# Expert tile lists with full tiles first, and list padding written from ScalarE's queue inside the tile loop, in a fused graph-attention and mixture-of-experts kernel

## The reference

```python
x = x + gnn(layernorm(x), adj, a0, a1, a2, a3)        # x is [128, 128, 128] f32
x = x + ffn(layernorm(x), gate_w, gate_b, w1, w2, w3)

# gnn: e_k = leaky_relu(einsum('bid,bjd->bij', h * a_k, h), 0.2); alpha takes e_k where adj == k + 1,
#      else -9e15; softmax over j; alpha @ h
# ffn: 16 experts, hidden 256
logits = einsum('bsd,de->bse', x, gate_w) + gate_b
probs = softmax(logits)
top_probs, top_idx = top_k(probs, 2)
top_probs = top_probs / sum(top_probs)
hidden = silu(x @ w1[e]) * (x @ w2[e])                # for each chosen expert e
out = sum over the two chosen e of top_prob_e * (hidden @ w3[e])
```

## Time and profile before

| | |
|---|---|
| median of 3 runs | 967.29 us (967.28 to 970.02) |
| the profiled execution | 967.5 us |
| its span in the trace | 965.7 us |
| busy, share of the span | PE 78%, POOL 54%, DVE 65%, ACT 45% |
| mean granted TensorE clock | 0.92 of full |
| bytes moved | 160.39 MB |

### The profile page before, as it was taken

The page is one execution under the profiler, slowest core; times in us unless marked ns, Lnnn a source line. Parts: engine busy times, 40 slices in busy tenths (PEclk is TensorE's granted clock), DMA queues, the critical chain, the costliest instruction groups (busy, mean ns, idle before and its releaser), DMA issues.

```text
span 965.7 us, 17975 instructions
## 1 busy us (share of the span) xinstructions
PE 748.7 (78%) x4233; PEld 594.5 (62%) x4233; DVE 624.6 (65%) x2534; ACT 438.3 (45%) x1090; POOL 521.3 (54%) x571
## 2 busy tenths in 40 slices
PE   2677677777777777420939999999959999999995
PEld 1344444444444444410729999888848999999995
DVE  2799999999999999740516666666533444444442
ACT  3687777777777777310303333333313333333331
POOL 2025555555555555550316666667654666766665
PEclk9899999999999999755869999999989999999998
DMA  3223333322222211113768878777728888888882
GB/s 104 72 82 100 99 100 100 100 83 70 68 67 68 67 56 35 33 46 91 250 240 269 281 272 271 250 264 259 245 84 272 271 265 273 275 267 269 270 268 86
DMA packets 134202, 160.39 MB, mean 166 GB/s; under 512 B 16985, under 2 KB 103263, under 8 KB 134144
## 3 DMA queue, kind: packets, MB, share of 16 engines
q1 hardware_dynamic: 117248, 125.37, 41.5%
q0 software_dynamic: 16896, 34.40, 10.5%
HBM read 55.53 MB, written 47.62 MB: 107 GB/s over the span
## 4 chain that ended last, share of the span: by engine, by line
SPq 38%; issue 13%; POOL 2%; DMA 2%; DVE 1%; PE 1%; ACT 0%; POOLq 0%; DVEq 0%
SPq L331 10%; SPq L328 9%; SPq L332 9%; SPq L329 7%; SPq L319 2%; SPq L320 2%; POOL second_list L425 1%; POOL out_dram L437 1%; POOL first_list L413 0%; DMA xin<-second_list 0%; PE bank L819 0%; DMA xin<-first_list 0%; DMA first_list<-padding 0%; SPq L326 0%; DMA first_list<-stage,slot 0%
## 5 line engine op out<-in xcount | busy, mean ns | idle before, releaser
L847 PE MATMUL psS<-xT,late 128*128 128x256 f32 x1280 | 308.4, 384 | 2.2 <-ACT xT L519 2.1
L847 PEld LDWEIGHTS psS<-xT,late 128*128 128x128 f32 x1280 | 234.0, 193 | 29.9 <-issue 2.0
L425 POOL DMA_INDIRECT second_list<-xin x160 | 156.9, 981 | 132.2 <-issue 66.3
L733 DVE TENSOR_TENSOR hid<-silu,psS 128x512 f32<-128x512 f32 x160 | 109.9, 687 | 161.5 <-PE psS L847 156.8
L437 POOL DMA_INDIRECT out_dram<-xin x160 | 156.5, 978 | 87.8 <-issue 66.5
L515 ACT ACTIVATE silu<-psS 128x512 f32<-128x512 f32 x160 | 95.5, 597 | 224.1 <-PE psS L847 224.1
L767 PE MATMUL psS<-late,hT 128*128 128x512 f32 x256 | 145.7, 721 | 44.5 <-ACT late L468 44.5
L868 PE MATMUL bank<-late,hid 128*128 128x128 f32 x1280 | 170.1, 276 | 0.1
L413 POOL DMA_INDIRECT first_list<-stage,slot x128 | 137.3, 1073 | 60.6 <-DVE stage L611 28.7
L868 PEld LDWEIGHTS bank<-late,hid 128*128 128x128 f32 x1280 | 156.5, 193 | 0.5 <-issue 0.4
L405 POOL TENSOR_TENSOR norm<-veps,minus_half 128x8 f32<-128x8 f32 (+1 forms) x36 | 55.5, 1541 | 154.9 <-DVE veps L584 154.9
(11 more groups left out here) (111 smaller groups left out, 820.3 us busy)
## 6 DMA issues: line engine op xcount, KB each, us to landing
late<-wts SPq DMA_DIRECT2D x160, 384.0 KB
xin<-second_list SPq DMA_DIRECT2D x80, 262.0 KB
xin<-first_list SPq DMA_DIRECT2D x80, 134.0 KB
X<-in_x_dram SPq DMA_DIRECT2D x32, 256.0 KB, 4.0
late<-in_adj_dram SPq DMA_DIRECT2D x32, 256.0 KB, 3.5
wts<-in_L_ffn_w_dram SPq DMA_DIRECT2D x48, 128.0 KB, 3.5
second_list<-padding SPq DMA_DIRECT2D x17, 262.0 KB, 3.0
second_list<-xin POOLq DMA_INDIRECT x160
```

What stands on the lines that cost most here:

```text
L425: pool.indirect_dma_start(second_list[:, :], bass.IndirectOffsetOnAxis(ap=xin[:, u, k, SLOT1:SLOT1 + 1].bitcast(i32), axis=0), xin[:, u, k ...
L733: v.tensor_tensor(hid[:, w, :], silu[:, w, :], psU[w], ALU.mult).then_inc(s_hid[u % TURNS], 1)
L847: last = mm(out[:, c * W2:(c + 1) * W2], we[:, u, half * H + c * P:half * H + (c + 1) * P], xT[:, w, :], start=True, stop=True)
```

## The change

Three things are changed together.

1. The tile table is made over 32 entries per list instead of 16: first the full tiles of all 16 experts (`count >> 8` of them each), then the 16 experts' ragged tiles, one each. Tiles without an expert follow as before. The sum of tiles is the same where no expert's count is a multiple of 256.
2. SP's queue no longer writes the ragged padding. The two IDLE transfers are issued near the start of the program. The 2 * 16 ragged ones are issued by ScalarE's queue, one after each tile's body: those of `first_list` in turns 1 and 2 of pass 1, those of `second_list` in turns 3 and 4. SP starts pass 1 without waiting for the padding, and waits for it before turn 6 (`sure` = 6, the number of turns that are made of full tiles whatever the counts are).
3. At the end of pass 1 SP's queue issues the weights of pass 2's first eight tiles, each as soon as its buffer's scatters have landed, and the rows of these eight tiles after the last of them.

```diff
-        def tiles(eng, body, ahead, r):
+        def tiles(eng, body, ahead, r, parts=()):
...
-            with eng.Fori(first // S + 1, end // S - 1) as n:
-                for u in range(S):
-                    body(n, u, lambda d: True)
+            at = first // S + 1
+            for upto_turn, what in (*parts, (end // S - 1, None)):
+                with eng.Fori(at, upto_turn) as n:
+                    for u in range(S):
+                        body(n, u, lambda d: True)
+                        if what:
+                            what(n, u)
+                at = upto_turn
...
+                if g == 0:
+                    sp.wait_ge(s_pad, 2)
+                    for r, rows, width in ((0, first_list, ROW), (1, second_list, ROW2)):
+                        sp.dma_start(rows[IDLE:IDLE + W2, :].rearrange("(p k) c -> p k c", k=2), padding[:, :, 0:width]
+                                     ).then_inc(s_padded[r], 16)
...
-            sp.wait_ge(s_padrow, 1)
-            pad(0, first_list, ROW)
+            sp.wait_ge(s_padded[0], 16)
+            sp.wait_ge(s_table, 1)
+            turns = TILES // S
+            for u in range(S):
+                load_rows(0, first_list, ROW, 0, u)
+                load_weights(0, 0, u)
+            sure = (TOKENS - E * (W2 - 1)) // W2 // S
+            load_tiles(0, first_list, ROW, 1, sure)
+
             sp.wait_ge(s_padded[0], (E + 1) * 16)
-            sp.wait_ge(s_table, 1)
-            load_tiles(0, first_list, ROW)
+            load_tiles(0, first_list, ROW, sure, turns)
 
             for u in range(S):
-                sp.wait_ge(s_z[u], TILES // S * 32)
+                sp.wait_ge(s_z[u], turns * 32)
+                load_weights(1, turns, u)
             sp.wait_ge(s_padded[1], (E + 1) * 16)
-            load_tiles(1, second_list, ROW2)
+            for u in range(S):
+                load_rows(1, second_list, ROW2, turns, u)
+            load_tiles(1, second_list, ROW2, turns + 1, TOP * turns)
...
-            for r in range(TOP):
-                tiles(act, tile, 1, r)
+            def pad_first(n, u):
+                row = act.value_load(padrow[0:1, 0, ds(n * S + u - S, 1)], min_val=0, max_val=ROWS1 - W2)
+                act.dma_start(first_list[ds(row, W2), :].rearrange("(p k) c -> p k c", k=2), padding[:, :, 0:ROW]
+                              ).then_inc(s_padded[0], 16)
+
+            def pad_second(n, u):
+                row = act.value_load(padrow[0:1, 1, ds(n * S + u - S - E, 1)], min_val=0, max_val=ROWS2 - W2)
+                act.dma_start(second_list[ds(row, W2), :].rearrange("(p k) c -> p k c", k=2), padding[:, :, :]
+                              ).then_inc(s_padded[1], 16)
+
+            act.wait_ge(s_pad, 2)
+            act.wait_ge(s_padrow, 1)
+            tiles(act, tile, 1, 0, ((1 + E // S, pad_first), (1 + 2 * E // S, pad_second)))
+            tiles(act, tile, 1, 1)
...
+            v.tensor_copy(sign[:, :, 1, :], sign[:, :, 0, :])
+            v.tensor_copy(start[:, :, 1, :], start[:, :, 0, :])
+            v.tensor_copy(skip[:, 0, :], zeroE[:, :])
+            v.tensor_copy(skip[:, 1, :], zeroE[:, :])
+            v.tensor_scalar(seq[:, 0, E:2 * E], zeroE[:, 0:E], 1.0, None, ALU.add)
+            v.tensor_scalar(seq[:, 1, E:2 * E], zeroE[:, 0:E], 1.0, None, ALU.add).then_inc(s_base, 1)
...
-            link(v.tensor_scalar(ntile_i[:, :, :], count[:, :, :], float(W2 - 1), None, ALU.add))
+            link(v.tensor_scalar(full_i[:, :, :], count_i[:, :, :], W2.bit_length() - 1, None,
                                  ALU.arith_shift_right))
-            link(v.tensor_copy(ntile[:, :, :], ntile_s[:, :, :]))
+            v.tensor_copy(seq[:, :, 0:E], full_i[:, :, :])
+            v.tensor_copy(skip[:, :, E:2 * E], full_i[:, :, :])
...
+            link(v.tensor_tensor(within2[:, :, :], within[:, :, :], skip[:, :, :], ALU.add))
...
```

More of the change, by code:

```diff
@@ L119, in gnn_then_moe @@
         count = sb("count", [P, TOP, E])
[L120 to L126, removed]
-        tileno = sb("tileno", [P, 1])
[L128 to L135, removed]
+        count_i = sb("count_i", [P, TOP, E], i32)
+        full_i = sb("full_i", [P, TOP, E], i32)
+        seq = sb("seq", [P, TOP, 2 * E])
+        skip = sb("skip", [P, TOP, 2 * E])
+        zeroE = sb("zeroE", [P, 2 * E])
+        entry = sb("entry", [P, 2 * E])
+        sign = sb("sign", [P, TOP, 2, E])
+        start = sb("start", [P, TOP, 2, E])
+        upto = sb("upto", [P, TOP, 2 * E])
+        tileno = sb("tileno", [P, 1])
+        past = sb("past", [P, TOP, 2 * E])
+        behind = sb("behind", [P, TOP, 2 * E])
+        within = sb("within", [P, TOP, 2 * E])
+        within2 = sb("within2", [P, TOP, 2 * E])
+        within3 = sb("within3", [P, TOP, 2 * E])
+        within4 = sb("within4", [P, TOP, 2 * E])
+        mine = sb("mine", [P, TOP, 2 * E])
+        myrow = sb("myrow", [P, TOP, 2 * E])
+        myexp = sb("myexp", [P, TOP, 2, E])
+        which = sb("which", [P, TOP])
         idle = sb("idle", [P, TOP])
@@ new lines, in tile_row, with load_rows, load_weights @@
+            def tile_row(r, j):
+                return sp.value_load(table_i[0:1, 1, r, ds(j, 1)], min_val=0, max_val=(ROWS2 if r else ROWS1) - W2)
+            def load_rows(r, rows, width, n, u):
+                row = tile_row(r, n * S + u - r * TILES)
+                sp.dma_start(xin[:, u, :, 0:width], rows[ds(row, W2), :].rearrange("(k p) c -> p k c", p=P)
+                             ).then_inc(s_in[u], 16)
+            def load_weights(r, n, u):
+                e = sp.value_load(table_i[0:1, 0, r, ds(n * S + u - r * TILES, 1)], min_val=0, max_val=E - 1)
+                sp.dma_start(we[:, u, :], wts[:, ds(e * EW, EW)]).then_inc(s_we[u], 16)
@@ L339, in load_tiles @@
+            def load_tiles(r, rows, width, first, end):
+                with sp.Fori(first, end) as n:
                     for u in range(S):
-                        load_tile(n, u)
-            sp.wait_ge(s_pad, 2)
+                        sp.wait_ge(s_z[u], n * 32)
+                        sp.sem_inc(s_turn, 1)
+                        load_rows(r, rows, width, n, u)
+                        load_weights(r, n, u)
             for i in range(SB):
@@ L693, in link @@
                 dve.wait_ge(s_mid, links[0])
[L695 removed]
+            both = [P, TOP, 2 * E]
+            first = (slice(None), slice(None), 0, slice(None))
+            dve.wait_ge(s_base, 9)
             dve.wait_ge(s_count, 1)
[L697 to L699 removed]
@@ L717, in _ @@
-            v.tensor_scalar(table[:, 0, :], texp[:, :], float(E - 1), None, ALU.min)
-            link(v.tensor_tensor(within3[:, :, :], within2[:, :, :], start[:, :, :], ALU.add))
-            link(v.tensor_tensor(myrow[:, :, :], within3[:, :, :], mine[:, :, :], ALU.mult))
+            link(v.tensor_tensor(within2[:, :, :], within[:, :, :], skip[:, :, :], ALU.add))
+            v.tensor_scalar(idle[:, :], which[:, :], 2.0 * E - 0.5, None, ALU.is_gt)
+            v.tensor_tensor(mine[:, :, :], entry[:, :].unsqueeze(1).to_broadcast(both),
+                            which[:, :].unsqueeze(2).to_broadcast(both), ALU.is_equal)
@@ L758, in _ @@
             pe.wait_ge(s_small, 6 * 16)
-            pe.wait_ge(s_base, 7)
+            pe.wait_ge(s_base, 9)
             def step(s, on):
```

48 lines of the change are left out of this document (27 added, 21 removed).

## The result

The changed kernel takes 935.71 us (median of 4 runs, 935.04 to 936.20) against 968.65 for the kernel before beside it (967.28 to 973.98). The ratio is 0.9643, 95% interval 0.9613 to 0.9673. The profiled execution has a span of 934.3 us, 31.4 less than the 965.7 of before. The forecast was 931.0 in 923 to 946, that is 0.962: inside the interval.

A forecast was written before the change was run, and what follows sets the result against it. TensorE bounds the tile passes, so only holes can gain; SP's queue is nearly a second bound. 967.5 - 24.6 - 19.1 + 5.5 + 1.2 + 0.7 = 931.2, in terms of the median 931.0 us, range 923 to 946.

The forecast's parts named there:

- Hole 1: Ahead of pass 1's first tile, SP issues 17 padding transfers and waits for them; taking them off SP gives -24.6 us.
- Hole 2: Behind pass 1's first eight tiles, SP issues second_list's padding; taking it off SP gives -19.1 us.
- ScalarE's issues: 32 padding issues in pass 1's tiles use 1.3 of 2.1 us free per tile on ScalarE: cost 0.
- The table: Before pass 1, the longer tile table ends near 429.0 us, over 1 us before the scatters have landed: cost nothing.
- Between the passes: Pass 2's first row load waits behind the last weight copy's register load and issue: +1.2 us (0 to +2.5).
- Start: VectorE makes six more small instructions before the first group: +0.7 us (0 to 1.2).
- The transfers beside tiles: Padding shares the DMA engines with pass 1's tiles: 4.5 us in turns 3 and 4, 1 for scatters, +5.5 us.
- rival A: Padding costs its full engine time, +18.7 us, or ScalarE's issues hold SP's queue up: 944 us, chance 0.17.
- B: Rival: the padding is free, nothing is lost in pass 1: 925.7 us, chance 0.13.
- C: Rival: padding issues block ScalarE's queue, making silu and `xT` late in 32 tiles: 974 us, chance 0.04.
- D: Rival: the wait before pass 1 stays, held by the scatters' landing or the table: 956 us, chance 0.03.
- a remainder of 2.9 us: Late rows in pass 1, from SP's queue pace, cost about 2.9 us and were left as they are.

The follow-up runs named there:

- tiny issues: The changed kernel with a register load and a 536-byte scratch DMA per tile added on ScalarE in turns 5 and 6 of pass 1, 16 in all: 936.60 us.
- the order alone: The new table with full tiles first and early IDLE transfers, ragged padding back on SP's queue, against the kernel before: 969.83 us, ratio 1.0007.
- the repeat: The changed kernel run again unaltered: 935.51 us, ratio 0.9648 to the kernel before.
- packed kernel: The changed kernel with a tile's row and expert packed into one number, one register load per tile on SP instead of two: 923.69 us.
- packed kernel with the scratch transfers: The changed kernel with one packed register load per tile, plus 16 scratch transfers of 262 KB in turns 5 and 6: 928.67 us.

## Why the prediction was right, and where not

*Hole 1:* -24.6 forecast, 24.64 measured from the last scatter to the first tile. (The prediction gives 434 to 458 us as slices 18 and 19; that is slice 19 alone, and no term rests on it.) *Hole 2:* -19.1, and no hole is left. *ScalarE's issues:* 0, and TensorE never waits for it in these turns; the tiny issues confirm it. *The order:* no change of the time, as the run with the order alone shows, though its profile has more late tiles. *The table:* it ends at 430.54 + 0.68 = 431.2, 0.5 us behind the issue of the last scatter (I had given it 0.9), and SP's first row load goes out at 434.26: hidden, as forecast.

*Between the passes:* +1.2 forecast, +1.34 and 2.0 in two profiles, and undoing it gave 1.25 back in the gap. The mechanism is the one given. The time of the run without it cannot show 1.3 us, since its interval is 3 us wide to each side. For the number of tiles at the lower clock I had no term; it is one or two, 2.2 us apart, from one execution to the next.

*Start:* +0.7 forecast; the first group begins 0.54 us later (8.78 against 8.24). The 2.6 us at the end of the first stage in the first profile are mostly of that execution.

*The transfers beside tiles:* +5.5 forecast, +7.0 measured (8.6 in the repeat). The size was near, the step was wrong, so the agreement is luck. It read: in turns 3 and 4 a tile needs 3.03 us of the engines, of which 0.97 can be used, so 3.12 us per tile. The mean there is 3.13, but made of 2.94 in turn 3 and 3.31 in turn 4. The packed kernel does those turns at 2.84 with the same transfers, at a share of 1.02 and 359 to 363 GB/s. A share of 0.97 or 1.00 was not the limit; the time of one transfer, read while it ran nearly alone, does not add up to the time of two that run together. What set the pace in its place stands in rival A: SP's queue, which was written there to have no slack. But the form given there was wrong too, since the queue is not held by ScalarE's issues (issue durations as before; tiny issues free) but by its own register loads, which summed to 6.6 to 9.1 us in turns 1 to 4 against 5.6 before. Of the rule that descriptor generation is locked between two issuing engines (the Trainium skill, Perfetto Trace Analysis, § DMA Instruction — HWDGE (DVE, Sync)) the trace shows no cost: SP's issue of a row load reads 386 ns at the median beside ScalarE's in turns 1 to 4 and without (one of 32 reads 1126 in the repeat). B, C and D did not occur.

What I read and did not follow: that a turn took SP's queue 23.21 us where TensorE needs 22.72. I took it as a remainder of 2.9 us that stays as it is, "since SP loses no more per turn than before". That premise failed: the queue's turns became 23.5 to 26.1 us. It was the second bound, and the late tiles that pass 1 of the changed kernel has came out there.

## What to carry to other kernels

Where an issuing queue's time per tile comes within a few per cent of the bound engine's, treat it as a bound of its own: added traffic can slow its register loads and shows up as late data. Before blaming the DMA engines, take one register load per tile off the queue with the transfers left alone, and see whether the queue then waits for buffers; here that was worth 8 to 12 us of 936, at least a quarter of what the whole change gained. Moving work out of a hole into a loop costs what the loop's second bound makes of it: the 7.0 us that were lost here went with one register load less and the same traffic.

## What the runs showed of the hardware

- A register load from SBUF on SP's queue took 262 ns at the least and often about 270. The 16 of a turn summed to 5.6 us at 272 to 282 GB/s (before, turns 2 to 4), to 6.0 to 6.9 at 256 to 263 (turns 5 to 8), and to 7.1, 8.5, 6.6 and 9.1 beside the padding, at 298, 308, 335 and 342. So they lengthen beside traffic, but the rate alone does not tell by how much. The packed kernel's single one read 948 ns (median, up to 1249) beside 360 GB/s and 280 to 656 (medians of the turns 1 to 8) in pass 2, where no padding ran.
- The issue of a row load stayed near 386 ns at the median throughout. That of a weight copy was 500 in the changed kernel and 1.1 us in turns 4 to 6 of the packed kernel with the scratch transfers, at 359 to 360 GB/s.
- A DMA share of 0.99 to 1.02 in a window is not the limit by itself: it was read at 310, 337, 344, 359 and 363 GB/s.
- Between the passes TensorE is idle for 9.4 to 12.2 us and comes back at a granted clock of 0.50 (692.28 to 697.04 in the changed kernel). In 7 of the 13 profiles one tile's matmuls run so (3.54 to 3.75 us instead of 1.89), in 6 two tiles' do, about 2.2 us apart. The idle time does not order them: two after 9.4, one after 12.2. The first stage's end moved by 4.9 us over the same profiles, with a granted clock of 0.84, 0.85 or 0.93 in the window from 24 to 100 us.
